# Linear attention's rows added and normalised one group further ahead, its first gathers in the layer before, and an earlier root in the second projections

## The reference

```python
x = x + ga * _L0_attn_ref(layernorm(x) * (1 + ca) + sa, ...)
x = x + gb * _L0_ffn_ref(layernorm(x) * (1 + cb) + sb, ...)   # top 2 of 16 experts: sum of p_k * row_k
# layer 1
h = layernorm(x) * (1 + ca) + sa
q, k, v = relu(h @ Wq.T) + EPS, relu(h @ Wk.T) + EPS, h @ Wv.T     # per head
kv_cum = cumsum(k outer v);  k_cum = cumsum(k)
out = (q @ kv_cum) / (q . k_cum + EPS)
x = x + ga * out @ Wo.T
x = x + gb * _L1_ffn_ref(layernorm(x) * (1 + cb) + sb, ...)        # softmax attention + mixture
```

## Time and profile before

| | us |
|---|---|
| median of 3 runs | 3682.87 |
| lowest and highest | 3681.88 and 3696.22 |
| profiled execution | 3690.43 |
| its span in the profile | 3688.7 |
| mean granted TensorE clock | 0.946 of full |

### The profile page before, as it was taken

How to read it: one execution, slowest core, us unless ns; L and a number is a source line. 1 busy time by engine, 2 the same in 40 slices (tenths; PEclk the granted TensorE clock), 3 DMA queues, 4 the chain that set the end, 5 groups by cost and what they waited for, 6 DMA issues and landing times. The chain is left out here.

```text
span 3688.7 us, 74382 instructions
## 1 busy us (share of the span) xinstructions
PE 3422.1 (93%) x29745; PEld 1573.6 (43%) x29746; DVE 3024.4 (82%) x3971; ACT 2545.4 (69%) x4700; POOL 513.8 (14%) x405
## 2 busy tenths in 40 slices
PE   9899999999999998667878876999999999999998
PEld 5433333333333333556666544733333333333333
DVE  8899999999999992624556544299999999999993
ACT  3188888888888886323222222588788888888887
POOL 4410000000000000332221133034530011000001
PEclk9699999999999999788888887999999999999999
DMA  9452020211212002243000376533130212202001
GB/s 257 123 161 38 14 43 14 37 32 25 37 20 37 14 11 94 90 144 99 26 27 14 85 193 174 165 67 60 41 58 18 38 43 58 39 14 42 15 15 46
DMA packets 307729, 233.29 MB, mean 63 GB/s; under 512 B 206359, under 2 KB 258488, under 8 KB 302738
## 3 DMA queue, kind: packets, MB, share of 16 engines
q1 hardware_dynamic: 291076, 179.46, 21.6%
q0 software_dynamic: 14832, 47.79, 3.9%
q10 hardware_dynamic: 1504, 1.64, 0.1%
HBM read 126.49 MB, written 102.76 MB: 62 GB/s over the span
## 5 line engine op out<-in xcount | busy, mean ns | idle before, releaser
L901 ACT ACTIVATE att_l_probs<-att_l_s_ps 128x512 f32<-128x512 f32 x4096 | 2214.1, 595 | 320.0 <-PE att_l_s_ps L831 253.3
L920 DVE TENSOR_REDUCE att_in_part_max<-att_l_max_ps 128x2 f32<-128x1024 f32 x1952 | 2328.6, 1218 | 18.8 <-PE att_l_max_ps L819 16.1
L846 PE MATMUL att_l_o_ps<-att_l_probs,att_l_v_sb 128*17 128x256 f32 x16384 | 1275.5, 386 | 1.1 <-ACT att_l_probs L901 1.1
L831 PE MATMUL att_l_s_ps<-att_in_q_sb,att_in_k_sb 50*128 50x512 f32 x2048 | 759.9, 447 | 9.5 <-DVE att_l_o_ps L937 9.0
L831 PE MATMUL att_l_s_ps<-att_in_q_sb,att_l_k_sb 50*128 50x512 f32 x2048 | 745.5, 449 | 0.4
L819 PE MATMUL att_l_max_ps<-att_l_k_sb,att_in_q_sb 50*128 50x512 f32 x2048 | 728.1, 446 | 1.1 <-DVE att_in_part_max L920 1.1
L819 PE MATMUL att_l_max_ps<-att_in_k_sb,att_in_q_sb 50*128 50x512 f32 x1856 | 666.0, 448 | 0.8 <-DVE att_in_part_max L920 0.8
L846 PEld LDWEIGHTS att_l_o_ps<-att_l_probs,att_l_v_sb 128*17 128x17 f32 x16384 | 278.4, 95 | 723.4 <-issue 389.1
L831 PEld LDWEIGHTS att_l_s_ps<-att_in_q_sb,att_in_k_sb 50*128 50x128 f32 x2048 | 312.2, 186 | 445.2 <-ACT att_l_probs L901 410.8
L831 PEld LDWEIGHTS att_l_s_ps<-att_in_q_sb,att_l_k_sb 50*128 50x128 f32 x2048 | 309.2, 185 | 438.3 <-ACT att_l_probs L901 397.5
L819 PEld LDWEIGHTS att_l_max_ps<-att_l_k_sb,att_in_q_sb 50*128 50x128 f32 x2048 | 292.4, 185 | 7.7 <-DVE att_in_part_max L920 7.7
(11 more groups left out here) (262 smaller groups left out, 2878.4 us busy)
## 6 DMA issues: line engine op xcount, KB each, us to landing
att_in_q_sb<-q_hi SPq DMA_DIRECT2D x256, 64.0 KB
slot_rows<-att_l_zeros POOLq DMA_DIRECT2D x10, 1024.0 KB, 15.7
ffn_parts<-slot_rows SPq DMA_DIRECT2D x40, 256.0 KB
...
att_in_q_sb<-q_lo SPq DMA_DIRECT2D x128, 72.0 KB
...
```

The lines of the kernel that those rows point to most:

```text
L831: nc.tensor.matmul(s_ps[:, c % SB], k_sb[j // GPB % 2][rows, pair, u * P:(u + 1) * P], q_sb[rows, j % QR, pair], start=True, stop=True).th ...
L846: last = nc.tensor.matmul(o_ps[32 * h:32 * h + AUG, cols], v_sb[:, j // GPB % 2, u, h * AUG:(h + 1) * AUG], probs[:, u % 2, h, cols], star ...
L901: nc.scalar.activation(probs[:, u % 2, h], s_ps[:, c % SB], ACT.Exp, scale=float(HD) ** -0.5).then_inc(exp_done, 1)
L920: nc.vector.reduce_max(part_max[:, j % 2, k], max_ps[:, r], AX.X).then_inc(slot_taken, 1)
```

## The change

It has four parts. In `finish_layer0`, POOL gathers group 1's rows too, behind group 0's and in the same place, into the first half of batch element 1's part of `z_all` (`next_got2`), and the stage ends only when all sixteen are in. In `linear_attention`, DVE adds rows and takes statistics for group n + 2 in group n's tail, and normalises group n + 1 in tile 0; POOL gathers for groups 2 to 7, always after the low parts; ACT takes the root at the start of a group; groups 6 and 7 are written out on DVE, since they add nothing. In `project_layer1_ffn`, ACT's root and modulation and PE's transposes of the first group stand ahead of the wait for the loads, POOL's `set_shift_rows` waits until the first group is normalised, and the bias is split later.

```diff
@@ finish_layer0, gpsimd
-            for t in range(TPG):
-                for k in range(2):
-                    nc.gpsimd.indirect_dma_start(
-                        out=m.next_got[:, t, k], out_offset=None, in_=io.slot_out[0:SLOTS // B],
-                        in_offset=bass.IndirectOffsetOnAxis(ap=m.get_at[:, 0, k, t:t + 1], axis=0),
-                        bounds_check=SLOTS // B - 1, oob_is_err=False).then_inc(next_rows, 16)
+            for n, got in enumerate((m.next_got, m.next_got2)):
+                for t in range(TPG):
+                    for k in range(2):
+                        nc.gpsimd.indirect_dma_start(
+                            out=got[:, t, k], out_offset=None, in_=io.slot_out[0:SLOTS // B],
+                            in_offset=bass.IndirectOffsetOnAxis(ap=m.get_at[:, 0, k, n * TPG + t:n * TPG + t + 1], axis=0),
+                            bounds_check=SLOTS // B - 1, oob_is_err=False).then_inc(next_rows, 16)
             pool.wait_ge(next_lo, KH)
-            pool.wait_ge(next_rows, 16 * 2 * TPG)
+            pool.wait_ge(next_rows, 16 * 4 * TPG)
@@ linear_attention, gpsimd
-            for tile in range(TPG, NT):
+            for tile in range(2 * TPG, NT):
                 t = tile % TPG
                 if t == 0:
-
-                    if tile > TPG:
-                        low_parts(tile // TPG - 2)
+                    low_parts(tile // TPG - 2)
                     pool.wait_ge(row_added, 2 * tile)
@@ linear_attention, scalar
                 part_heads(n)
+                if not last_one:
+                    ln_root(nc, act, m, ln, n + 1)
                 for t in range(1, TPG):
                     copy_kv(n * TPG + t, t)
                     copy_sums(n * TPG + t - 1)
-                if not last_one:
-                    ln_root(nc, act, m, ln, n + 1)
                 copy_sums(n * TPG + TPG - 1)
@@ linear_attention, vector
-                            dve.wait_ge(rows_in[t], 32 * n)
+                            dve.wait_ge(rows_in[t], 32 * (n - 1))
...
-                    if t == TPG - 1 and not last_one:
-                        ln_normalize(nc, dve, m, ln, n + 1, tile, lambda: None)
...
                     if t > 0:
                         divide(n, t - 1)
-                    if t < 2 and not last_one:
-                        add_rows(n + 1, b_next, tile, t)
-                    if t == 2 and not last_one:
-                        dve.wait_ge(row_added, (n + 2) * 2 * TPG)
-                        ln_stats(nc, dve, m, ln, n + 1, tile)
+                    if t == 0 and not last_one:
+                        ln_normalize(nc, dve, m, ln, n + 1, tile, lambda: None)
                 divide(n, TPG - 1)
+                if ahead:
+                    b_ahead, tile_ahead = group_behind(b, q, 2)
+                    add_rows(n + 2, b_ahead, tile_ahead, 0, got)
                 if not last_one:
                     relu(K_HALVES, n + 1, 0)
+                if ahead:
+                    add_rows(n + 2, b_ahead, tile_ahead, 1, got)
+                    dve.wait_ge(row_added, (n + 3) * 2 * TPG)
+                    ln_stats(nc, dve, m, ln, n + 2, tile_ahead)
+                if not last_one:
                     relu(Q_HALVES, n + 1, 2)
                 wo_vector(nc, dve, m, wo, n)
...
             dve.wait_ge(loaded, 48)
+            add_rows(1, 0, TPG, 0, m.next_got2, first=True)
             relu(K_HALVES, 0, 0)
+            add_rows(1, 0, TPG, 1, m.next_got2, first=True)
             relu(Q_HALVES, 0, 2)
+            dve.wait_ge(row_added, 4 * TPG)
+            ln_stats(nc, dve, m, ln, 1, TPG)
...
-                with dve.Fori(0, GPB - (b == B - 1)) as q:
+                with dve.Fori(0, GPB - 2 * (b == B - 1)) as q:
                     group(b, q)
-            group(B - 1, GPB - 1, last_one=True)
+            group(B - 1, GPB - 2, ahead=False)
+            group(B - 1, GPB - 1, last_one=True, ahead=False)
@@ project_layer1_ffn, gpsimd
             pool.wait_ge(ones_set, 3)
+            pool.wait_ge(z_ready, TPG)
             set_shift_rows(nc, ai.k[0], ai)
@@ project_layer1_ffn, tensor
+            turn_normed(0)
             pe.wait_ge(loaded, 16 * 8)
-            pe.wait_ge(ones_set, 3)
-            turn_normed(0)
...
                 if n == GPB:
+                    pe.wait_ge(ones_set, 3)
                     count(0)
@@ project_layer1_ffn, scalar
-            act.wait_ge(loaded, 16 * 8)
             root(0)
             modulate(0)
-            act.wait_ge(bias_set, 2)
-            act.wait_ge(bias_loaded, 32)
-            for row in (0, BROWS // 2):
-                nc.scalar.activation(bias[row:row + 1], b_raw[row:row + 1], ACT.Copy).then_inc(bias_hi, 1)
+            act.wait_ge(loaded, 16 * 8)
...
                     modulate(n + 1)
+                if n == 0:
+                    act.wait_ge(bias_set, 2)
+                    act.wait_ge(bias_loaded, 32)
+                    for row in (0, BROWS // 2):
+                        nc.scalar.activation(bias[row:row + 1], b_raw[row:row + 1], ACT.Copy).then_inc(bias_hi, 1)
@@ project_layer1_ffn, vector
-                if n == 0:
+                if n == 1:
                     low = slice(BROWS // 2, BROWS // 2 + 1)
```

16 lines of the change are left out of this document (9 added, 7 removed).

## The result

The changed kernel took 3645.89 us, median of 4 runs (3644.10 to 3650.15); the kernel before 3684.71 (3681.88 to 3696.22). The profiled execution took 3645.60 us, its span 3643.8.

A forecast was written before the change was run, and what follows sets the result against it. TensorE, busy 93% of the span, was taken as the bound. Terms 9.0 - 2.9 - 25.2 + 13.0 + 3.0 - 6.1 = -9.2 us gave 3674 us from the median of 3682.87; range 3650 to 3692.

The forecast's parts named there:

- The bound and the block: TensorE bounds the kernel; in layer 0's block, eight more gathers stall the items, +9.0 us, bounds 7.9 and 10.5.
- Rival D: Layer 0's block: the second eight gathers are absorbed like the first, costing 1.3 us; 3666 us, chance 0.08.
- First group: Linear attention's start: low parts are split before the gathers, so `project` no longer waits 2.90 us; -2.9 us.
- VectorE's group: Linear attention's tile loop: adds and statistics move out, saving 3.6 us in each of seven groups; -25.2 us.
- Rival B: Tile loop: PE does not take up what VectorE gives, half of 25.2 lost; 3686 us, chance 0.10.
- Where the burst falls: Six bursts move to group tails, where PE sets the end; each costs 8 us instead of 5.84, +13.0 us.
- Shared access: Group tails: first adds run beside POOL's low parts and slow on shared SBUF access; 0.5 us each, +3 us.
- The root: Start of second projections: ACT's root no longer waits for loads, and normalisation avoids POOL's memset; -6.1 us.
- A: Linear attention: a burst costs the same 5.84 us wherever it stands, with no lock; 3658 us, chance 0.27.
- C: Group tails: the burst holds up the next group's chain of hand-overs, 12.5 us each; 3703 us, chance 0.09.

The follow-up runs named there:

- e2: Kernel before the change with the linear attention's seven gather bursts and the waits for them left out; chip 14, 3652.51 us, ratio 0.9898.
- e1: Changed kernel with the linear attention's six gather bursts and the waits for them left out; chip 14, 3633.60 us, ratio 0.9849 to the kernel before.
- e17: Changed kernel run again without edits on chip 14; 3657.52 us, ratio 0.9916 to the kernel before.
- e4: Changed kernel with each burst held back until the mask of the next group's tile 0 is done; chip 14, 3673.66 us, ratio 0.9961 to the kernel before.
- e18: Changed kernel with each burst held back until the next group's tile 0 mask, run in a later series on chip 14; 3680.54 us, ratio 0.9968.

## Why the prediction was wrong

**The bound and the block: right.** The second eight gathers cost the block 10.3 us between e2 and e1 on one chip, and 10.3 in the first pair too, counted from the first gather on (12.5 with what came ahead of it); the term was +9.0 with bounds of 7.9 and 10.5. Rival D is out where the delay exists.

**First group: right.** From the first add to the first mask it was 27.9 us and is 24.35; 24.5 in e2, which has no burst there. The term was -2.9, and the two rounds of adds and the statistics that moved there cost nothing, as forecast.

**VectorE's group: right.** -25.2 was the term; 23.7 us lie between e2 and e1, 25.3 without the last group, and group 6 takes 34.73 us where "about 35.0" stood. The split was another: 0.79 us a group, 5.5 in all, was put down to the clock, and 10.9 us came from faster work of PE. Rival B is out.

**Where the burst falls: this step failed.** The prediction said "6 x (8 - 5.84) = +13.0", since in the tail "the engine that sets the end is PE and VectorE has no backlog to work off", and took 2.9 off for the first group. Together +10.1 was forecast for all bursts. Measured is 38.1 us for seven before and 17.2 to 26.7 for six after: -11.4 to -20.9; by the medians of chip 14 alone it is 23.9 - 38.5 = -14.6. A burst after the change costs 2.9 to 4.5 us, not 8.

The argument took a busy PE for one that cannot afford a wait, and carried PE's whole loss of before, 4.71 us of wait and 2.3 at half clock, rounded up to 8, into the tail. In the trace PE runs on for 8.3 us of the tail's burst with work that it can start, and is idle for 2.92 + 0.50 us under the rest. Over the six bursts PE's added idle time is 12.5 us in the first trace and 18.3 in e17, 2.1 to 3.1 a burst, and its work takes 6.3 and 11.4 us longer, 1.1 to 1.9 a burst, at a granted clock of 0.97 and 0.95 and not 0.99. The sentence that each burst "now starts when the second adds of the tail are done" also misread the new list of POOL: the first of the six does not.

That the place sets a part of the price is shown, by e4 and e17 at the same clock and by e18 beside e17. Why one place is dearer is argued: in the tile loop more hand-overs fall under a burst than PE's own work covers, and e18's rows show at least four late ones. That only the late part of a burst delays, as the expectation of e1 had it, does not hold: in e18 ACT is held up by work that was ready 1.6 us into the burst.

**Shared access: mis-sized the other way round.** The adds do take twice as long, the full 1.7 to 1.8 us; the price in time was nearly nothing (a group without burst, with adds, takes 35.07 in e1, one without adds 34.73), and +3 was forecast.

**The root: right**, -6.0 for -6.1.

**Rivals.** A (3658 us) had the right direction of the error and not the size: not only did the burst not grow dearer, it grew cheaper. C's condition, a chain of hand-overs each held up by the burst, holds for e18's place in the tile loop; in the tail the relu and the parted queries came in time, and two hand-overs were late, of which PE waited for one.

The sum with measured terms: +12.5 - 23.7 - 20.9 - 6.0 = -38.1, against -38.8. On chip 14 the medians of e1 and e2 give -18.9 for all but the bursts, and with -14.6 for these -33.5, against 32.8 measured by e17. So part of the miss is one of the execution and the chip: the same kernel's gain was 32.8 to 38.8 us on chips with the delay. Taken off the 3682.87 that the range was built on, chip 14's gain gives 3650.1, just inside; the failed step is the same.

What stays open: what delays the messages on some chips, and why PE's clock fell for longer in one execution than in another of the same kernel on the same chip (e4 and e18, 341.9 and 351.3 us). The chip of the first two traces is not on record, so that 361.9 and 317.2 are of chips with the delay is read from their blocks alone.
